# Retention layer with a quantized linear branch: the first group's instructions in another order

## What is computed

```python
xn = _layernorm(x, axis=-1)
# retention, 16 heads of 64
q = heads((x @ Wq + bq) * scaling); k = heads(x @ Wk + bk); v = heads(x @ Wv + bv)
ret = einsum('bhid,bhjd->bhij', q, k) * D[None]      # D: decay ** (i - j), causal
ret = ret / clip(abs(ret.sum(-1)), 1.0, None)
attn = einsum('bhij,bhjd->bhid', ret, v)
g = (attn - mean) / sqrt(var + EPS) * gn_w + gn_b    # per head
y = silu(x @ Wg + bg) * g @ Wo + bo
# linear with block-quantized (fp4) input and weight
wq, ws, w_tensor_scale = quantize_nvfp4(weight)      # tensor scale: max of the whole weight
xq, xs, _ = quantize_nvfp4(x2d, x_tensor_scale)
out = x + y + einsum('mbk,nbk->mn', xq * xs, wq * ws) * (x_tensor_scale * w_tensor_scale) + bias
```

## Time and profile before

| what | value |
|---|---|
| median of 3 runs | 2232.05 us (2230.95 to 2232.88) |
| the profiled execution | 2231.07 us |
| its span, first to last instruction | 2228.9 us |
| mean granted TensorE clock | 0.972 |
| PE busy | 2093.5 us (94%) |
| DVE busy | 1534.4 us (69%) |
| ACT busy | 689.3 us (31%) |
| POOL busy | 641.3 us (29%) |
| DMA queue of SP | 268.19 MB |

### The profile page before, as it was taken

One profiled execution on the slowest core, in us unless ns is written; L12 is line 12 of the kernel. 1 busy time (PEld: TensorE's weight loads), 2 busy tenths in 40 slices (PEclk: granted clock), 3 DMA queues, 4 the chain that ended last, 5 costly groups with the idle time before them and its releaser, 6 DMA issues.

```text
span 2228.9 us, 51250 instructions
## 1 busy us (share of the span) xinstructions
PE 2093.5 (94%) x18047; PEld 1066.7 (48%) x18098; DVE 1534.4 (69%) x4379; ACT 689.3 (31%) x1318; POOL 641.3 (29%) x456
## 2 busy tenths in 40 slices
PE   5687888989899999999999999999999999999999
PEld 3343444444454545555545455554554555545444
DVE  8587878999966666666676766666666666666742
ACT  5555451322133223222322322223222322322210
POOL 1222232233232332223332232332332223323321
PEclk8888999999899999999999999999999999999999
DMA  7656733432333332323333233233333322333323
GB/s 309 214 190 219 258 110 95 144 108 91 94 119 118 101 106 90 100 89 104 118 110 109 90 99 108 77 118 118 108 108 90 99 90 94 119 118 99 104 75 123
DMA packets 180244, 269.30 MB, mean 121 GB/s; under 512 B 117184, under 2 KB 117312, under 8 KB 180160
## 3 DMA queue, kind: packets, MB, share of 16 engines
q1 hardware_dynamic: 180160, 268.19, 37.7%
HBM read 201.04 MB, written 37.75 MB: 107 GB/s over the span
## 4 chain that ended last, share of the span: by engine, by line
PE 74%; DVE 17%; DMA 3%; issue 2%; ACT 1%; SPq 1%; POOL 0%; DVEq 0%; ACTq 0%
PE mm L1257 46%; PE mm L1199 7%; PE tp L1199 7%; PE mm L1208 4%; DMA ftile<-in_w_f 2%; PE tp L1267 2%; PE four L1307 2%; PE four L1320 2%; PE tp L1295 1%; DVE xa L807 1%; PE four L1280 1%; DVE xa L808 1%; DVE state L1004 1%; DVE xa L802 1%; DVE wo L896 1%
## 5 line engine op out<-in xcount | busy, mean ns | idle before, releaser
L1257 PE MATMUL mm<-xnT,wring 128*128 128x512 f16 x6144 | 1379.2, 383 | 14.4 <-ACT qT L620 14.1
L1257 PEld LDWEIGHTS mm<-xnT,wring 128*128 128x128 f16 x6144 | 603.1, 99 | 720.3 <-issue 44.1
L651 ACT ACTIVATE work<-four,gs 128x64 f32<-128x64 f32 x512 | 158.5, 414 | 575.5 <-DVE gs L1031 575.5
L512 POOL TENSOR_TENSOR yT<-gn,gate 128x512 f32 (+1 forms) x64 | 82.8, 1293 | 881.2 <-ACT gn L662 881.2
L1018 DVE BATCH_NORM_STATS2 gst<-four 128x6 f32<-128x64 f32 x512 | 73.6, 217 | 215.4 <-PE four L1320 215.4
L1199 PE MATMUL mm<-wo,yT 128*128 128x512 f16 x864 | 194.1, 381 | 0.1
L495 POOL TENSOR_TENSOR qparts<-qT,qparts 128x512 f16<-128x512 f32 x64 | 78.5, 1227 | 372.0 <-ACT qT L620 371.8
L495 POOL TENSOR_TENSOR kparts<-kT,kparts 128x512 f16<-128x512 f32 x64 | 83.0, 1297 | 234.5 <-ACT kT L620 234.5
L1199 PE MATMUL tp<-wo,yT 128*128 128x512 f16 x672 | 149.6, 379 | 0.0
L1199 PEld LDWEIGHTS mm<-wo,yT 128*128 (+1 forms) x864 | 82.3, 98 | 98.7 <-issue 1.9
L620 ACT ACTIVATE vT<-mm,consts,down 128x512 f32<-128x512 f32 x64 | 49.8, 778 | 230.4 <-PE mm L1257 230.4
(11 more groups left out here) (194 smaller groups left out, 2710.5 us busy)
## 6 DMA issues: line engine op xcount, KB each, us to landing
wring<-parts SPq DMA_DIRECT2D x252, 512.0 KB, 3.5
xt<-in_x SPq DMA_DIRECT2D x34, 512.0 KB, 3.6
out<-res SPq DMA_DIRECT2D x32, 512.0 KB, 3.0
parts<-wo SPq DMA_DIRECT2D x28, 512.0 KB, 8.1
res<-in_x SPq DMA_DIRECT2D x28, 512.0 KB, 3.6
ftile<-in_w_f SPq DMA_DIRECT2D x16, 512.0 KB, 4.7
parts<-wring SPq DMA_DIRECT2D x8, 512.0 KB, 7.1
probs<-in_x SPq DMA_DIRECT2D x5, 512.0 KB, 3.8
```

The costliest lines, as they stand in the source:

```text
L512: nc.gpsimd.tensor_tensor(hi, gn[:], gate[:, u], ALU.mult)
L651: last = nc.scalar.activation(work[:, c * P + h * HD:c * P + (h + 1) * HD], ao[h][:, c * VW:c * VW + HD], ACT.Identity, bias=gs[:, 1, g:g ...
L1257: last = MM(mm[n % 2][:], wring[:, n, wj, k, :], xnT[:, parity, xj, k, :], start=(j == 0), stop=(j == 3 * KT - 1))
```

## The change

Nothing is added to or taken from the computation. What is changed is the order:

- The eight tiles of the linear weight go alternately to `ftile` and to `res` (the result tile, used in START for a bias and free after that until SECOND), with a semaphore for each. A load waits for the maximum of the tile two before. Bodies take tiles 0 | 1, then 2, 3 | 4, then 5, 6 | 7, then none; the first part is loaded behind the first two slices and reduced behind `states(0)`, the second is loaded behind the second pair's third slice and reduced at the end of the body. In SECOND the load into `res` waits for all maxima.
- In START the first sum goes between the second and the third transposed tile. The second goes behind `project(0, 0)` of body 0. Body 0's sum of batch 1 goes behind `project(1, 1)`.
- In bodies 1 to 3 DVE makes the weights' scales right behind the layer norm, and the low parts are spread in three parts (four, two, two) about the halves of the quantization. In body 0 the scales go behind the second half of the quantization.
- `transpose_g(0)` goes behind `attend_within(1)`.
- SP issues the fourth slice's load ahead of the transposing DMAs of x's parts (`move_x_parts`), and in bodies 1 to 3 `pass_on(range(0, 4))` ahead of both.

```diff
-F_TILES = ((0, 1, 2), (3, 4, 5), (6, 7), ())
+F_TILES = (((0,), (1,)), ((2, 3), (4,)), ((5, 6), (7,)), ((), ()))
...
+        f_in = [ctx.enter_context(nc.semaphore(f"f_in{j}")) for j in range(2)]
+        f_bufs = [ftile, res]
...
                 def load_f_raw(t):
-                    if t:
-                        sp.wait_ge(s["f_max"], at("f_max", START, 0, t))
-                    sp.dma_start(ftile[:], a["w_f"][t * P:(t + 1) * P, :]).then_inc(s["f_loaded"], 16)
+                    if t > 1:
+                        sp.wait_ge(s["f_max"], at("f_max", START, 0, t - 1))
+                    elif t == 1:
+                        sp.wait_ge(bias_sum, 1)
+                    sp.dma_start(f_bufs[t % 2][:], a["w_f"][t * P:(t + 1) * P, :]).then_inc(f_in[t % 2], 16)
...
                         load_slice(0, n)
+                    load_fs(F_TILES[i][0])
                     if i == 0:
                         load_raw(1, 6)
                         load_raw(1, 7)
-                    next_f()
                     load_slice(0, 2)
                     if i == 0:
                         for c in range(4, SLICES):
                             store_parts(0, c)
+                    else:
+                        pass_on(range(0, 4))
+                    load_slice(0, 3)
                     move_x_parts()
-                    load_slice(0, 3)
-                    if i > 0:
-                        pass_on(range(0, 4))
                     w("xq_ready", 1)
                     move_x()
...
                     load_slice(1, 0)
                     load_slice(1, 1)
-                    next_f()
                     pass_on(range(4, SLICES))
                     load_slice(1, 2)
-                    next_f()
+                    load_fs(F_TILES[i][1])
                     load_slice(1, 3)
                     return
+                if phase == SECOND:
+                    w("f_max", 0)
                 w("out_stored", 0)
                 sp.dma_start(res[:], a["x"][rows, :]).then_inc(s["res_loaded"], 16)
...
                     layernorm(xt[:])
                     w("xn_ready", 1)
-                    quantize_scales(xt, x_ts, x_r6)
-                    w("xq_moved", 0)
-                    quantize_half(xt, 0)
                     if i == CH - 1:
                         in_scales(weight_scales)
                     if i:
                         scale_batch()
-                        split_lo(i + 1, range(0, 6))
+                    quantize_scales(xt, x_ts, x_r6)
+                    w("xq_moved", 0)
+                    if i:
+                        split_lo(i + 1, range(0, 4))
+                    quantize_half(xt, 0)
+                    if i:
+                        split_lo(i + 1, range(4, 6))
                     mask_scores(0)
+                    if i:
+                        split_lo(i + 1, range(6, SLICES))
+                    quantize_half(xt, 1)
                     if i == 0:
                         scale_batch()
-                    quantize_half(xt, 1)
-                    if i:
-                        split_lo(i + 1, range(6, SLICES))
                     states(0)
-                    find_f_max()
+                    find_f_max(F_TILES[i][0])
                     if i == 0:
                         split_lo(1, range(0, 4))
                     group_norm(0)
-                    find_f_max()
...
                     group_norm(1)
-                    find_f_max()
+                    find_f_max(F_TILES[i][1])
...
             for t in range(CH):
                 w("xn_ready", t + 1)
+                if t == 2:
+                    pe.wait_ge(ones_set, 1)
+                    pe.wait_ge(s["xnT_ready"], 1)
+                    sum_slices(0, 0, 4)
                 for j in range(2):
...
-            pe.wait_ge(ones_set, 1)
-            pe.wait_ge(s["xnT_ready"], 1)
-            sum_slices(0, 0, 4)
-            pe.wait_ge(sums_read, 1)
-            sum_slices(0, 4, 4)
...
                 project(0, 0)
+                if phase == FIRST and i == 0:
+                    pe.wait_ge(sums_read, 1)
+                    sum_slices(0, 4, 4)
                 project(0, 1)
...
                 project(1, 0)
+                scores(0)
+                project(1, 1)
                 if phase == FIRST and i == 0:
                     pe.wait_ge(sums_read, 2)
                     sum_slices(1, 0, SLICES)
-                scores(0)
-                project(1, 1)
                 state_increments(0)
...
                 if phase == FIRST:
-                    transpose_g(0)
                     state_increments(1)
                     attend_within(1)
+                    transpose_g(0)
                     attend_earlier(1)
                     return
```

More of the change, by code:

```diff
@@ L90 @@
     "res_biased": (0, 0, 1, 1, 1), "out_ready": (0, 0, 1, 1, 1), "late_full": (0, 0, 0, 0, 2), "late_added": (0, 0, 0, 0, 2), "late_ready": (1, 0, 0, 0, 1),
-    "xqf_ready": (0, 0, 2, 0, 0), "xqf_moved": (1, 0, 2, 0, 0), "f_loaded": (0, 2, 2, 0, 0),
+    "xqf_ready": (0, 0, 2, 0, 0), "xqf_moved": (1, 0, 2, 0, 0), "f_loaded": (0, 0, 2, 0, 0),
     "xq_moved": (1, 1, 1, 1, 0), "x_moved": (1, 2, 2, 2, 0),
@@ L381, in body, with load_fs @@
                 if phase == FIRST:
-                    f_tiles = iter(F_TILES[i])
-                    def next_f():
-                        for f in f_tiles:
+                    def load_fs(tiles):
+                        for f in tiles:
                             load_f_raw(f)
-                            break
                     def pass_on(slices):
@@ L428, in body @@
                 if phase == SECOND:
-                    w("f_max", 0)
                     load_f(0)
@@ L949, in spread_f_max @@
             def spread_f_max():
+                dve.wait_ge(s["f_max"], at("f_max", SECOND, 0, 0))
                 in_scales(lambda: then(V.tensor_reduce(w_ts, maxs[:, FMAX:FMAX + KT], AX_X, ALU.max)))
@@ L1031, in group_norm, with find_f_max @@
                     V.scalar_tensor_tensor(m, m, -0.5, y, ALU.mult, ALU.mult).then_inc(s["gstats"], 1)
-                f_tiles = iter(F_TILES[i]) if phase == FIRST else ()
-                def find_f_max():
-                    for f in f_tiles:
-                        dve.wait_ge(s["f_loaded"], at("f_loaded", START, 0, f + 1))
-                        V.tensor_reduce(maxs[:, FMAX + f:FMAX + f + 1], ftile[:], AX_X, ALU.max,
+                def find_f_max(tiles):
+                    for f in tiles:
+                        dve.wait_ge(f_in[f % 2], 16 * (f // 2 + 1))
+                        V.tensor_reduce(maxs[:, FMAX + f:FMAX + f + 1], f_bufs[f % 2][:], AX_X, ALU.max,
                                         apply_absolute_value=True).then_inc(s["f_max"], 1)
-                        break
                 def scale_batch():
```

## The result

The changed kernel took 2207.78 us (median of 4 runs, 2205.46 to 2208.07), the kernel before beside it 2231.64 (2230.95 to 2232.88). The time lies 11 us above the forecast and 5 above the range that the forecast had for itself, 2191 to 2203; inside 2182 to 2210 it lies only because that range takes in the rival at 2207. The profiled execution took 2207.72 us, with a span of 2205.9.

A forecast was written before the change was run, and what follows sets the result against it. The first group was taken as bounded by DVE, meeting PE at the score masks. Terms 19.1 + 4.7 + 3.7 + 3.9 - 2.5 + 3.8 + 2.2 = 34.9 us gave 2197 us, range 2182 to 2210.

The forecast's parts named there:

- the rival at 2207: Rival in which the first group's three late tile loads wait longer, cutting the gain by 10.1 us; chance 0.15.
- START, 2.3: In START, moving the first sums lets q's projection start at 45.5 instead of 47.8: gain 2.3 us.
- Body 0, up to the second mask, 19.1 with START: Body 0: earlier slice load, moved sum and one tile fewer bring the second mask 19.1 us earlier, START's 2.3 included.
- Tiles, 9.1 + 1.2 and 4.7 + 3.7: Tile waits go: body 0 saves 9.1 us and a 1.2 us maximum, bodies 1 and 2 save 4.7 and 3.7.
- The loads bind: Rival: late tiles 1, 4, 7 wait 9.1 for 5.8 and 4.7 for 1.3 twice; 2207 us, chance 0.15.
- Transposing g later, 2.2 in body 3: Body 3: g transposed behind the within-products frees the state increments from ACT, gaining 2.2 us.
- Early scales, 3.9 and 3.4 of body 3's 3.8: Bodies 1 to 3: scales right behind the layer norm remove DVE's waits for ACT's halves, 3.9 and 3.4 us.
- The scales aren't early: Rival: a late sum of products stops DVE at the scales, so 7.3 us of waits stay; 2204 us, chance 0.1.
- More goes: Rival: tiles 4 and 7 never wait and port blocks in three bodies fall on idle time; 2182 us, chance 0.12.
- Slower: Rival: the fourth slice's load on SP's queue in bodies 1 to 3 lands 18 to 25 us late; 2237 us, chance 0.02.

The follow-up runs named there:

- e8: Changed kernel with one extra 1.2 us VectorE reduction, result unused, behind body 3's last group norm; 2205.59 us.
- e5: Changed kernel with VectorE's old order of scales and low parts in bodies 1 to 3; 2200.69 us.
- e11: Changed kernel with VectorE's old order in bodies 1 to 3 and both first sums back in front of the first projection; 2205.46 us.
- e6: Kernel before with only the linear weight's tiles changed (two alternating buffers, new places of loads and maxima); 2221.25 us.
- e4: Changed kernel with the first pair's transposed g back in front of the state increments; 2201.82 us.
- e9: Changed kernel with VectorE's old order in bodies 1 to 3 and the transposed g back in front of the state increments; 2206.02 us.
- e12: Changed kernel with VectorE's old order in bodies 1 to 3, the same kernel as e5 measured on another occasion; 2200.15 us.
- e10: Changed kernel with body 0's sum of batch 1 and its fourth slice's load back in their old places; 2212.1 us.
- e2: Kernel before with POOL's gating instructions in the first group cut from 512 to 32 columns; 2222.62 us.
- e3: Changed kernel with the first pair's transposed g moved behind the second products with the states (attend_earlier(1)); 2206.97 us.
- e7: Changed kernel with both of START's first sums back in front of the first projection; 2205.27 us.
- e1: Changed kernel with POOL's gating instructions in the first group cut from 512 to 32 columns; 2193.27 us.

## Why the prediction was right, and where not

Reading the second group's layer norm of e8 less its added 1.2 as that of the changed kernel without the low clock gives 296.3: a gain of 25.1 in the first group, where the sum said 34.9. On the way, in us:

| gain up to | forecast | e8 | forecast without early scales | e5 |
|---|---|---|---|---|
| second mask of body 0 | 19.1 | 19.1 | 19.1 | 18.7 |
| second mask of body 1 | 25.8 | 23.5 | 23.8 | 25.5 |
| second mask of body 2 | 31.4 | 27.3 | 27.5 | 30.4 |
| second group's layer norm | 34.9 | 25.1 | 27.6 | 27.6 |

- **START, 2.3: right.** The projection began at 30.20 (said 30.7), q's at 45.94 (said 45.5). e5 against e11 puts it at 2.25 at the first mask (and at 4.0 at the end of the group, more than the sum had). First mask: said 62.9, e8 has 62.13.
- **Body 0, up to the second mask, 19.1 with START: right.** e8 has 108.23 - 89.14 = 19.1. The load was issued at 59.00 instead of 66.51, and undoing this part costs 9.1 at the first mask, where I had 7.4, and 7.5 over the group, where I had 6.5. That the parts meet at 19.1 exactly is in part luck.
- **Tiles, 9.1 + 1.2 and 4.7 + 3.7: the waits went.** Behind the last statistics tile 1 still waits 3.8 (4.7 in e8), tile 7 0.8 and tile 4 not at all (0.8 in e8), less than I had set (5.8, 1.3, 1.3). *The loads bind* wanted 9.1 and 4.7 there and was wrong. But e6 shows that this term doesn't stand by itself: 15.4 at the second mask of body 1, and 5.7 at the end of the group.
- **Transposing g later, 2.2 in body 3: not so in the changed kernel.** There body 3 is 1.1 longer for it and the whole group 0.7 shorter (e8 against e4); in e5's order body 3 is 1.2 and the group 3.0 shorter (e5 against e9). The wait of 8.8 was kept from showing, as said. I didn't see that it had hidden the gates. Moving it bared 8.9 of blocks.
- **Early scales, 3.9 and 3.4 of body 3's 3.8: wrong, and in size this is the whole of the miss.** The waits for halves went. In the step behind them I said "Before, four quantization instructions bore this; now the scale chain does, so DVE's sum is unchanged". It was not: DVE's instructions became 7.3 longer, and 2.9 of other waits came. The quantization was not relieved as the scale chain was loaded, since POOL's splits and decays lengthened it where the gates no longer did. Against e8 corrected, 296.3, e5 and e12 (293.83, 294.49) put early scales at -2.5 and -1.8, where I had +7.3. That is 9.1 to 9.8 of the 9.8 missing.
- **That the rest of the sum is right does not follow.** Without this term the forecast is 27.6, and e5 has 27.6, e12 26.9; but the table shows e5 2.9 ahead of it at body 2's second mask and losing that behind, where two errors cancel. In body 3 alone I had 6.0 for early scales and g, and e8 has 1.4 (62.47 before, 61.07). What made e5's bodies 1 and 2 quicker than the sum stays open.
- *The scales aren't early* was not it: the scales were early, and the sum stopped them once, in body 1, for 2.03 us (1.1 in e8), about the 1 or 2 us of that rival. Its time, 2204, is near the measured one for another reason.
- *More goes* counted on blocks of 4 us a body falling on idle time. The opposite came: idle time that had covered blocks went.
- *Slower* and *The loads bind*: the fourth slice's load shows in no wait of PE.

The Trainium skill (SBUF — State Buffer, Who interferes with whom) has the rule by which this goes: a VectorE instruction with two SBUF inputs contends with a GpSimd instruction that reads SBUF, for one lock, so it waits the other out. The trace agrees at 118.16, as above. I drew on it and took the wrong sum from it: I compared one burst (3.0 before, 3.1 after, and there I was right), not the seven, and none of POOL's other work.

Behind the first group nothing was gained or lost, 1907.5 in both, as I had taken it. This was luck: in the other twelve runs the same code took 1899.1 to 1907.2. PE's second group starts at 291.39 (said 281.6).

**A better version.** e5 beats both kernels: the change with DVE's old order in bodies 1 to 3, 2200.7 and 2200.2 us in two measurements, 0.986 of before. How much of its 7 us is its own is less sure than that it is there: 2 to 5 lie in the first group, 4 or 5 behind it, where the instructions are the same.

## What to carry over

A wait of one engine can be the cover under which another runs instructions that would block it. Before you count a wait as a gain, look at what POOL does in it, and where these instructions will fall when it is gone: here four bursts moved from idle time onto DVE's work for 7.9 us of its busy time. And when you move instructions out from under one of POOL's, look at which of its others they come to stand beside. Where something must stand beside POOL's gates, one instruction is caught for each of POOL's, and a 0.15 us instruction pays 1.0 us as well; longer ones came off a little better here (6.5 against 8.6 us in three bursts). Test a moved step by undoing it alone, since the parts of this change don't add (10.2 us for the tiles alone, -2 for the early scales inside the whole).

## What was unexpected

The stretch from the second group's layer norm to the end has the same code in all kernels but takes 1907.5 us before and after, 1903.5 in e4, e5, e6 and e9, 1902.7 in e10, and 1904.9 to 1907.2 in e2, e3, e7, e8 and e11. It repeats in the same kernel (1903.5 and 1902.6 for e5 and e12). Nearly all of the difference lies in the second group alone: from its first layer norm to the third group's it takes 294.8 us in the changed kernel, 290.8 in e5 and 286.5 in e1, and what follows takes 1612.7, 1612.6 and 1612.6. DVE's busy time in it, for the same instructions, is 267.9, 265.1 and 261.5. The same count as above puts 51.2, 48.4 and 44.8 us of it down to instructions lengthened beside POOL's, and none to others. So most of the difference is again how DVE and POOL meet. What decides it stays open, since e8's delay moved it by 1.0 alone. It means that a single kernel's total carries some 4 us that its edit didn't earn; e8's total and the last 4 us of e4, e5 and e6 are of that kind.

The clock after a wait of PE in START came back at different speeds in otherwise equal executions (q's projection 5.34 or 6.98 us at a granted 1.00 or 0.76).
